# Queries projected transposed in a transformer stage on one NeuronCore: rotary halves exchanged and inverse norms spread by transfers

## The reference, cut to what matters

```python
q, k, v = split(shift(x) @ Wqkv[i])          # 16 heads of 64
q = l2norm(q) * q_scale ; k = l2norm(k) * k_scale
q = q * cos * scale + rotate_half(q) * sin * scale
k = k * cos / scale + rotate_half(k) * sin / scale
x = local_attention(q, k, v) @ Wo[i] + x     # windows of 32 tokens, own and previous
x = ffn(shift(x)) + x                        # layer norm, gated GELU, width 341
```

## Time and profile before

| | us |
|---|---|
| median of 3 runs (lowest to highest) | 4251.59 (4249.69 to 4258.62) |
| profiled execution, own time | 4247.64 |
| its span | 4245.5 |
| transformer stage, from its first projection | from 972 to the end |
| one pass in the steady state | about 33 |

### The profile page before, as it was taken

The page is one execution under the profiler, slowest core; times in us unless marked ns, Lnnn a source line. Parts: engine busy times, 40 slices in busy tenths (PEclk is TensorE's granted clock), DMA queues, the critical chain, the costliest instruction groups (busy, mean ns, idle before and its releaser), DMA issues.

```text
span 4245.5 us, 144543 instructions
## 1 busy us (share of the span) xinstructions
PE 4079.6 (96%) x63655; PEld 2975.9 (70%) x63655; DVE 3294.3 (78%) x6965; ACT 2414.7 (57%) x4394; POOL 2229.2 (53%) x1351
## 2 busy tenths in 40 slices
PE   6999999896999999999999999999999999999997
PEld 4767777673677777777777777777777777776775
DVE  4344444356888888888888888888888888889995
ACT  3010111144667767676676766767767677666664
POOL 2011011025666666666666666666666666666662
PEclk8999999998999999999999999999999999999998
DMA  4111111000111111111111111111111111111110
GB/s 155 40 60 41 40 60 41 20 1 25 37 40 37 51 46 42 41 37 51 46 42 41 37 50 47 42 41 37 51 46 45 38 37 51 46 43 40 45 39 26
DMA packets 76231, 186.16 MB, mean 44 GB/s; under 512 B 15819, under 2 KB 44630, under 8 KB 71126
## 3 DMA queue, kind: packets, MB, share of 16 engines
q1 hardware_dynamic: 74870, 176.51, 13.5%
q10 hardware_dynamic: 736, 0.40, 0.0%
HBM read 61.25 MB, written 2.36 MB: 15 GB/s over the span
## 4 chain that ended last, share of the span: by engine, by line
PE 66%; DVE 5%; ACT 3%; issue 1%; POOL 1%; DMA 0%; DVEq 0%; POOLq 0%; SPq 0%
PE pQ L1666 15%; PE pTO L1699 9%; PE pS L1650 9%; PE pM L1734 7%; PE pTO L1712 7%; PE pM L1723 7%; PE pC L1768 6%; PE pTO L1680 3%; PE pC L1778 3%; ACT sq L1531 2%; ACT pS L1515 1%; DVE rot L1380 1%; DVE m L1384 1%; DVE n L1395 1%; POOL rot L1298 1%
## 5 line engine op out<-in xcount | busy, mean ns | idle before, releaser
L1298 POOL TENSOR_TENSOR rot<-rot,m 128x1024 f32<-128x1024 f32 x384 | 905.4, 2358 | 385.6 <-DVE m L1384 385.6
L1290 POOL TENSOR_TENSOR rot<-rot,rn 128x1024 f32<-128x1024 f32 x384 | 733.0, 1909 | 280.7 <-DVE rn L102 280.7
L1531 ACT ACTIVATE sq<-pQ 128x1024 f32<-128x1024 f32 x380 | 389.5, 1025 | 438.0 <-PE pQ L1666 437.7
L1307 POOL TENSOR_TENSOR E<-E,rc 128x512 f32<-128x512 f32 x384 | 400.7, 1044 | 349.1 <-DVE rc L1370 348.8
L1699 PEld LDWEIGHTS pTO<-PT,V 64*64 64x64 f32 x24576 | 401.8, 134 | 108.5 <-issue 99.8
L1380 DVE TENSOR_TENSOR rot<-pQ,tabl 128x1024 f32<-128x1024 f32 x380 | 456.7, 1202 | 12.1 <-ACT sq L1531 9.9
L1384 DVE TENSOR_TENSOR m<-pQ,tabl 128x1024 f32<-128x1024 f32 x380 | 461.2, 1214 | 0.1
L1650 PEld LDWEIGHTS pS<-kT,qT 64*32 64x32 f32 x24576 | 361.7, 107 | 140.5 <-issue 105.8
L1395 DVE TENSOR_REDUCE n<-sq 128x16 f32<-128x1024 f32 x380 | 459.2, 1208 | 0.0
L1650 PE MATMUL pS<-kT,qT 64*32 64x64 f32 x24576 | 426.6, 218 | 25.1 <-issue 15.5
L1699 PE MATMUL pTO<-PT,V 64*64 64x32 f32 x24576 | 444.2, 221 | 4.0 <-ACT PT L1540 2.5
(11 more groups left out here) (226 smaller groups left out, 6973.9 us busy)
## 6 DMA issues: line engine op xcount, KB each, us to landing
V<-V SPq DMA_DIRECT2D x192, 384.0 KB, 3.5
b_cB<-b_crow SPq DMA_DIRECT2D x32, 1024.0 KB, 6.3
xs<-XT SPq DMA_DIRECT2D x192, 64.0 KB, 2.9
V<-V SPq DMA_DIRECT2D x96, 128.0 KB, 3.3
ys<-XT SPq DMA_DIRECT2D x192, 64.0 KB, 2.2
wq<-in_wqkv SPq DMA_DIRECT2D x6, 512.0 KB, 4.3
wk<-in_wqkv SPq DMA_DIRECT2D x6, 512.0 KB, 4.4
wv<-in_wqkv SPq DMA_DIRECT2D x6, 512.0 KB, 5.6
```

The lines of the kernel that those rows point to most:

```text
L1290: e.tensor_tensor(r, r, rn[b % 2][:, c:c + HEADS].unsqueeze(2).to_broadcast([P, HEADS, HD]), ALU.mult)\
L1298: e.tensor_tensor(rot[j % RING][:, :], rot[j % RING][:, :], m2[:, :, :].rearrange("p h d -> p (h d)"), ALU.add)\
```

## The change

Queries are projected with features on partitions: the weights are the stationary operand, and each piece u = 0, 1 holds 4 blocks of 128 features x 256 tokens. So they need no turning. Keys and values stay as they were. For the queries:

- ACT squares pQ as before and copies it into `rot` (`copied`).
- The halves of a head now lie on different partitions, so four DMAs per piece exchange them into `rsw` (`swap`, 32 partitions x 4 KB each).
- DVE multiplies `rot` and `rsw` in place by tables (`cosine`, `sine`), both operands in SBUF; POOL adds them.
- Norms come from PE: `norms` multiplies the squares with a 128 x 32 selector, 16 matmuls of 64 columns per piece, in four column groups, into a new bank pN. `roots` now handles 96 columns and has one more instruction.
- The inverse norms go to DRAM (`write_rows`, 32 KB) and come back spread over partitions (`spread`, two DMAs of 256 KB per piece) into `rb`; POOL multiplies `rot` by `rb` straight into qT.
- Four PE transposes and one ACT copy fewer for each of the four query half-banks; one bank pM is left where there were two, handled by halves.
- The keys' sine product goes to `rsw` in place of `m2`; the ring of `rot` buffers has six in place of five. All five engines' lists are in a new order. Ten constant loads replace four; the query table is transposed at the start of the stage. The 16 first sequences are turned through pC.

```diff
-    RING = 5
+    RING = 6
...
+        rb = [sb(f"rb{i}", [P, 4, L]) for i in range(2)]
+        nrow = [nc.dram_tensor(f"nrow{i}", (P, NQ), F32).ap() for i in range(2)]
+        rsw = [sb(f"rsw{i}", [P, N]) for i in range(2)]
...
-        pM = [ps("pM0", [P, 512]), ps("pM1", [P, 512])]
+        pM = ps("pM", [P, 512])
+        pN = ps("pN", [P, 512])
...
+                for a in range(4):
+                    b = a ^ 1
+                    e.dma_start(rsw[u][a * HD // 2:(a + 1) * HD // 2, :], rot[j % RING][b * HD // 2:(b + 1) * HD // 2, :])\
+                        .then_inc(swap_l[u], 16)
...
+                e.dma_start(nrow[n % 2], rn[n % 2][:, 0:NQ]).then_inc(row_l, 16)
...
+                for x in range(2):
+                    src = nrow[n % 2].rearrange("(j i x) k -> i j (x k)", j=4, i=2)[x:x + 1, :, u * L:(u + 1) * L]
+                    e.dma_start(rb[u][x * HD:(x + 1) * HD, :, :], src.to_broadcast([HD, 4, L])).then_inc(rb_l[u], 16)
...
+                swap(A, 0)
+                swap(A, 1)
+                write_rows(A)
+                next_xs(A)
+                spread(A, 0)
+                query_weights(A)
+                spread(A, 1)
+                ffn_weights(C)
+                next_ys(Dn)
+                shift_values(R, 0)
+                store(F)
...
+                if u < 2:
+                    e.wait_ge(rb_l[u], 32 * (n + 1))
+                    if u == 0 and n >= 2:
+                        e.wait_ge(p_s.sem, p_s.at("s", 4 * (n - 2) + 3))
+                    e.wait_ge(g_add.sem, g_add.at("add", j))
+                    e.tensor_tensor(qT[n % 2][:, 4 * u:4 * u + 4, :], r[:, :].rearrange("p (j l) -> p j l", l=L), rb[u][:, :, :], ALU.mult)\
+                        .then_inc(g_rn.sem, 1)
...
             for A, R, B, Dn, C, F in passes():
+                root(C)
+                by_sum(B, 0)
                 unit_scale(R, 0)
-                root(C)
-                rotary_add(A, 0)
                 unit_scale(R, 1)
-                by_sum(B, 0)
-                rotary_add(A, 1)
                 unit_scale(R, 2)
                 last_root(F)
                 by_sum(B, 1)
+                rotary_add(A, 0)
+                rotary_add(A, 1)
                 unit_scale(R, 3)
+                by_sum(B, 2)
                 rotary_add(A, 2)
-                by_sum(B, 2)
+                rotary_add(A, 3)
                 by_sum(B, 3)
-                rotary_add(A, 3)
...
+                x = rot[j % RING][:, :].rearrange("p (j l) -> p j l", l=L)
+                e.tensor_tensor(x, x, tabq[:, 0, :].unsqueeze(1).to_broadcast([P, 4, L]), ALU.mult)\
+                    .then_inc(v_cos.sem, 1)
...
+                x = rsw[u][:, :].rearrange("p (j l) -> p j l", l=L)
+                e.tensor_tensor(x, x, tabq[:, 1, :].unsqueeze(1).to_broadcast([P, 4, L]), ALU.mult)\
+                    .then_inc(v_sin.sem, 1)
...
+                e.tensor_scalar(n2[:, 0:NQ], pN[:, 0:NQ], 1e-24, None, ALU.max).then_inc(v_nt.sem, 1)
+                e.tensor_scalar(n2[:, NQ:NT], n2[:, NQ:NT], 1e-24, None, ALU.max).then_inc(v_nt.sem, 1)
...
+                statistics(C)
                 if A is not None and starts(A):
                     tables(A)
                 less_max(B, 0)
-                statistics(C)
-                rotate(A, 0)
                 normal(C)
-                squares(A, 0)
+                sums(B, 0)
                 less_max(B, 1)
-                sums(B, 0)
-                rotate(A, 1)
-                squares(A, 1)
                 roots(A if A is not None else NP if R == NP - 1 else None)
+                sine(A, 0)
                 last_stats(F)
+                cosine(A, 0)
+                sums(B, 1)
                 attention_add(Dn)
+                cosine(A, 1)
                 less_max(B, 2)
-                sums(B, 1)
+                sine(A, 1)
+                rotate(A, 2)
+                squares(A, 2)
+                sums(B, 2)
                 hidden(C, 0)
-                rotate(A, 2)
                 less_max(B, 3)
-                squares(A, 2)
-                last_normal(F)
-                sums(B, 2)
                 hidden(C, 1)
                 hidden(C, 2)
+                rotate(A, 3)
+                squares(A, 3)
+                ffn_add(C)
+                last_normal(F)
                 sums(B, 3)
-                rotate(A, 3)
-                ffn_add(C)
-                squares(A, 3)
...
+                e.activation(rot[j % RING][:, :], projected(j)[:, :], ACT.Copy).then_inc(a_raw.sem, 1)
...
                 square(A, 0)
+                copied(A, 0)
+                probs(Dn, 3)
                 masked(B, 1)
-                probs(Dn, 3)
-                turned(R, 0)
                 exponent(B, 0)
+                square(A, 1)
+                copied(A, 1)
+                affine(C)
                 heads_out(Dn, 3)
-                square(A, 1)
+                values(R, 0)
+                exponent(B, 1)
                 masked(B, 2)
-                values(R, 0)
-                affine(C)
-                exponent(B, 1)
                 gelu(C, 0)
                 gelu(C, 1)
                 probs(B, 0)
                 square(A, 2)
-                turned(R, 1)
+                values(R, 1)
+                heads_out(B, 0)
+                turned(R, 2, 0)
+                masked(B, 3)
                 gelu(C, 2)
-                masked(B, 3)
-                heads_out(B, 0)
-                turned(R, 2)
+                turned(R, 2, 1)
+                probs(B, 1)
                 exponent(B, 2)
-                probs(B, 1)
-                values(R, 1)
+                values(R, 2)
+                heads_out(B, 1)
+                square(A, 3)
+                values(R, 3)
                 exponent(B, 3)
-                square(A, 3)
-                heads_out(B, 1)
-                turned(R, 3)
                 probs(B, 2)
+                turned(R, 3, 0)
+                turned(R, 3, 1)
                 if B is not None and B + 1 < NP:
                     masked(B + 1, 0)
                 heads_out(B, 2)
...
+                for i in range(0 if w else 4):
+                    c = 4 * t + i
+                    x = e.matmul(projected(j)[:, i * L:(i + 1) * L], wqkv[w][:, c * P:(c + 1) * P], xs[n % 3][:, 0:L], start=True, stop=True)
...
+                for b in range(4):
+                    for i in range(4):
+                        x = e.matmul(pN[32 * i:32 * i + 32, 0:NQ], sel[:, 32 * (4 * u + b):32 * (4 * u + b + 1)],
+                                     squared(j)[:, i * L + b * L // 4:i * L + (b + 1) * L // 4], start=(b == 0 and u == 0),
+                                     stop=(b == 3 and u == 1), skip_group_check=True, tile_position=(0, 32 * i))
...
-                scores(B, 0)
                 project(A, 0)
                 back(C)
+                scores(B, 0)
+                norms(A, 0)
                 probs(Dn, 3)
-                turn(R, 0)
+                project(A, 1)
+                normed(C)
                 scores(B, 1)
+                norms(A, 1)
                 attend(Dn, 3)
-                project(A, 1)
+                hidden(C, 0)
                 values(R, 0)
-                normed(C)
+                probs(B, 0)
+                last(F)
                 combine(Dn)
-                probs(B, 0)
-                hidden(C, 0)
-                last(F)
                 project(A, 2)
                 scores(B, 2)
-                turn(R, 1)
+                values(R, 1)
+                attend(B, 0)
+                turn(R, 2, 0)
                 hidden(C, 1)
-                attend(B, 0)
-                turn(R, 2)
+                probs(B, 1)
+                turn(R, 2, 1)
                 scores(B, 3)
-                probs(B, 1)
-                values(R, 1)
+                values(R, 2)
+                attend(B, 1)
                 project(A, 3)
+                values(R, 3)
                 hidden(C, 2)
-                attend(B, 1)
-                turn(R, 3)
                 probs(B, 2)
+                turn(R, 3, 0)
                 contract(C)
                 attend(B, 2)
+                turn(R, 3, 1)
```

More of the change, by code:

```diff
@@ new lines, in next_ys, with swap @@
+            def next_ys(n):
+                if n is None:
+                    return
+                fetch_ys(n)
+                if starts(n + 1) and n + 1 < NP:
+                    e.dma_start(wo[:, :, :], I["wo"][(n + 1) // NSEQ, :, :, :]).then_inc(wo_l, 16)
+            def swap(n, u):
+                if n is None:
+                    return
+                j = 4 * n + u
+                e.wait_ge(a_raw.sem, a_raw.at("cp", own(j)))
+                if n:
+                    e.wait_ge(g_add.sem, g_add.at("add", j - 2))
+                for a in range(4):
+                    b = a ^ 1
+                    e.dma_start(rsw[u][a * HD // 2:(a + 1) * HD // 2, :], rot[j % RING][b * HD // 2:(b + 1) * HD // 2, :])\
+                        .then_inc(swap_l[u], 16)
```

(48 more changed lines are left out.)

305 lines of the change are left out of this document (190 added, 115 removed).

## The result

| | before | after |
|---|---|---|
| median, us | 4250.98 (4 runs) | 4802.59 (4 runs, 4799.63 to 4807.91) |
| ratio, 95% interval | | 1.1302 [1.1288, 1.1317] |
| span of the profiled execution | 4245.5 | 4801.2 |
| mean granted clock of TensorE | 0.986 | 0.943 |

The change costs 552 us, twice the 276 of the forecast, and the time lies above the range. The page's busy times answer to the earlier trace rows, then come the DMA packets (before: 76231 packets, 186.16 MB, 44 GB/s), two of its queues, and the two new transfers.

The account below looks back on a forecast made before the run. PE was taken to bound the kernel before; after, DVE's waits for POOL lengthen 92 passes by 3.0 us each to 36.2: 4248 + 276 = 4524 profiled, 4528 us as median; range 4290 to 4720, 8 in 10.

Parts of the forecast that it names:

- PE's own work: PE's work in a pass after the change: 32.3 us, or 32.7 with new waits on PE.
- The walk: DVE's instructions followed through one pass, then PE to the next project(A, 0): 36.2 us a pass.
- Its waits for POOL: DVE waiting in roots (1.7, 2.4), cosine(A, 0) (1.9), cosine(A, 1) (0.75) and sine(A, 1) (1.0): 7.75 us a pass.
- The work between them: Work and short idling in the pass outside the waits for POOL: 28.45 us.
- The rule of which engine goes next: DVE instructions with two SBUF operands and POOL's take turns; whichever asks while the other works goes next.
- All this costs nothing: The new DMA traffic, 2.1 MB more a pass, and SP's later loads cost nothing while late by less than 5 us.
- The clock: Rival: PE's clock falls in its new idle stretches, 37.5 to 39.5 us a pass, 4650 to 4840 us; 13%.
- The first rival: The shared port does not hold DVE up; PE's 32.7 us a pass rules, 4211 us, faster; 10%.
- norms one by one: Rival: norms runs one instruction at a time, PE 35.7 us; near 4490 us without waits for POOL; 5%.
- half the waits: Rival: DVE's waits for POOL are only 3.5 to 6 us, pass 32.8 to 34.5, 4220 to 4380 us; 17%.

Follow-up runs that it names:

- x1: The changed kernel with the next layer's feed-forward and key weights issued first on SP, ahead of everything that waits: 4716.9 us.
- w2: x1 with the spreading reading the same bytes in 4 KB runs in place of four 1 KB runs: 4583.0 us.
- y1: x1 with, after the first unit, the exchange cut to one column a partition and the spreading to one element: 4576.3 us.
- y2: y1 with five matmuls of unused result (2.15 us) on PE before attend(B, 0): 4533.9 us.
- w1: y1 with the queries' sine and cosine products replaced by one-operand sums over the rows: 4316.4 us.
- x3: The changed kernel with POOL's list reordered: unit_scale(R, 0) before the roots, by_sum(B, 0) behind both unit_scales: 4732.4 us.
- y4: w1 with POOL's order of x3: 4376.3 us.
- y3: x1 with transfers in full and the queries' sine and cosine products replaced by one-operand sums: 4634.4 us.
- x2: The changed kernel with five matmuls of unused result (2.15 us) on PE before attend(B, 0): 4823.1 us.

## Why the prediction was wrong

The sum by runs, each step one edit but where two are named (parts are rounded; in another order of the steps they would differ somewhat):

| step | from | to | us |
|---|---|---|---|
| weights behind the roots on SP | after | x1 | 86 |
| 1 KB pieces of the spreading | x1 | w2 | 134 |
| all other traffic of the two transfers | w2 | y1 | 7 |
| the clock, from PE's idle before attend(B, 0) | y1 | y2 | 42 |
| products waiting for POOL (two edits: w1 has no filler either and needs none) | y2 | w1 | 217 |
| PE's own work and waits that stay | w1 | before | 65 |
| | | | 552 |

- **The walk: right.** 36.02 for 36.2. Its waits for POOL: 1.35 for 1.7, 2.1 for 2.4, 1.7 for 1.9 (2.92 less 1.22), 0.8 for 0.75, 0.8 for 1.0; together 6.75 for 7.75. The work between them is 29.3 and not 28.45, so the sum came out by two small errors of opposite sign. The last two lines of the table, 283 us, are the forecast's 276. The rule of which engine goes next, taken from the earlier trace rows, holds at each of these places.
- **The step that failed: "All this costs nothing", of the DMAs.** It compared bytes and landings with the room of the DMA engines, and both were as it said: swaps land in 2.3 us, and the exchange is free. It failed in two other ways. The list of what is queued behind the roots on SP had xs and ys in it and left out the feed-forward and key weights, which have nothing ahead of them to hide in once a layer: 86 us. And it priced the spreading by bytes; 98,304 pieces of 1 KB delay PE's own instructions: 134 us, from x1 to w2. Stalls fall by 70 us (94.5 to 24.4), and the lower clock by 126 (351.6 to 225.3), which at half speed is worth up to 63: by this estimate the two are the whole.
- **The clock: a rival with too small a chance.** The mechanism was as described from the earlier trace rows, at the place and with nearly the idle (2.4 for 3 us) that the forecast named. It gave 13% for one fall in each pass at 1.3 to 3.3 us each. By itself, in y1, it happens in six passes of ten and costs 0.9: 42 us.
- **PE's own work: sized too small.** norms take 0.58 a piece (0.52 forecast, lower bound 0.26, upper 2.0), and PE is busy 32.8 and not 32.3 us in w1. Under a walk of 36 it did not matter. The first rival, 4211 and faster as soon as the waits for POOL sum to under 4.2 us, is not reached where they do: in w1 only the roots' 3.45 us are left, the pass is 33.55 and not 32.7, and the median 4316. Beside PE's own work there is the wait of attend(B, 0) for its bank; waits for POOL were not free up to that sum.
- **norms one by one, half the waits:** both excluded, by 0.58 and by the timelines above.

The three costs that were left out, or held unlikely, all act on PE from outside the pass's dependences: a load that comes once a layer, the supply of instructions, the clock. In the profile of before the loads and the clock cost nothing in a steady pass, and the 15 stalls, 15.5 us in 95 intervals, are too few to be seen in one pass, so a walk along its waits could not find them.

## What to carry to other kernels

When an instruction on a DMA queue begins to wait for a late result, list every issue behind it, those that occur once a layer too, and put what waits for nothing first. Count the pieces of a transfer that repeats small rows, not its bytes: w2 saves 134 us with the same 391 MB. DVE instructions with two SBUF operands, and small tensor_scalars from SBUF, should be laid where GpSimd has nothing ready; moving one of its instructions away from one of them only moves the wait to the next (x3, y4).

## What the runs showed of the hardware that was not expected

- PE's instructions come in blocks of 256, one 16 KB packet each, and the stops inside a call, 0.3 to 4.7 us long, all end at the same place of a block. With the same pieces in flight there are more of them where DVE waits less: 60 in after, 89 in x3 and in y3.
- Adding 2.15 us of idle-filling matmuls to each pass made the kernel 42 us faster where nothing else stood in the way (y1 to y2), and 20 us slower with the pieces, the stalls and the late loads there (after to x2).
- A tensor_scalar of 2 columns waits for a GpSimd tensor_tensor as a wide one does: 1.92 for 0.17 us. A tensor_reduce of 1024 columns from SBUF does not: 1.21 us with and without it (w1).
